# Issuing the value products of two attention steps together, with four probability buffers

## The reference

```
q, k, v = split(x @ Wq.T + bq), split(x @ Wk.T + bk), split(x @ Wv.T + bv)
q_stp = q @ Wqs.T + bqs
cross_kv = cross(k @ Wks.T + bks, v @ Wvs.T + bvs)
scores = (einsum('bhqd,bhkd->bhqk', q, k) + einsum('bhqc,bhkc->bhqk', q_stp, cross_kv)) * temp
attn = softmax(scores, axis=-1)
out = einsum('bhqk,bhkd->bhqd', attn, v)
```

## Time and profile before

| | us |
|---|---|
| median of 3 runs | 3909.57 |
| the profiled execution | 3902.91 |
| its span, first to last instruction | 3900.8 |
| TensorE matmul busy | 3424.4 (88%) |
| VectorE busy | 2953.6 (76%) |
| ScalarE busy | 2202.5 (56%) |
| GpSimd busy | 1521.5 (39%) |

### The profile page before, as it was taken

The page is one execution under the profiler, slowest core; times in us unless marked ns, Lnnn a source line. Parts: engine busy times, 40 slices in busy tenths (PEclk is TensorE's granted clock), DMA queues, the critical chain, the costliest instruction groups (busy, mean ns, idle before and its releaser), DMA issues. The chain is left out here.

```text
span 3900.8 us, 50068 instructions
## 1 busy us (share of the span) xinstructions
PE 3424.4 (88%) x14561; PEld 1588.6 (41%) x14561; DVE 2953.6 (76%) x3565; ACT 2202.5 (56%) x3624; POOL 1521.5 (39%) x1294
## 2 busy tenths in 40 slices
PE   3238989898898979889988999999999999999898
PEld 1114545455454545546542333323323333333566
DVE  3898787887878788796337888888878888887343
ACT  3436455554646555463215777777777777776221
POOL 0988778787878887797100000000000000000110
PEclk8669999899999989999998999999999999999999
DMA  2111213122121311223301000000000000001010
GB/s 97 33 33 54 60 57 106 57 76 73 55 82 57 106 57 58 69 75 105 107 19 66 18 18 18 18 19 20 22 16 21 18 18 18 18 18 34 22 32 27
DMA packets 110809, 183.02 MB, mean 47 GB/s; under 512 B 14608, under 2 KB 84648, under 8 KB 101866
## 3 DMA queue, kind: packets, MB, share of 16 engines
q1 hardware_dynamic: 110569, 180.13, 14.7%
HBM read 153.99 MB, written 26.09 MB: 46 GB/s over the span
## 5 line engine op out<-in xcount | busy, mean ns | idle before, releaser
L1830 DVE TENSOR_REDUCE tile_max<-ps 128x1 f32<-128x1024 f32 x1028 | 1211.4, 1220 | 246.4 <-PE ps L1621 243.6
L1771 ACT ACTIVATE probs<-ps 128x512 f32<-128x512 f32 x2056 | 1116.1, 598 | 372.4 <-PE ps L1635 346.7
L1373 POOL TENSOR_TENSOR vals<-vals,c_sb 128x512 f32<-128x512 f32 x512 | 685.0, 1369 | 321.7 <-DVE state L1182 321.6
L1176 DVE TENSOR_TENSOR_SCAN vals<-stacks,state,ps 128x512 f32<-128x512 f32 x512 | 655.1, 1280 | 105.9 <-POOL heads_v L1384 36.1
L1635 PE MATMUL ps<-stacks 101*128 101x512 bf16 x2056 | 708.8, 383 | 3.0 <-ACTq L1778 1.7
L1384 POOL TENSOR_TENSOR heads_v<-heads_v,vals 128x512 f32<-128x512 f32 x512 | 638.4, 1278 | 8.7 <-issue 0.2
L1621 PE MATMUL ps<-stacks 99*128 99x512 bf16 x2056 | 615.3, 380 | 0.0
L1645 PE MATMUL ps<-probs,heads_v 128*32 128x512 f32 x4096 | 546.3, 605 | 3.5 <-issue 3.5
L231 POOL COPY heads_v<-vals 128x256 f32 (+1 forms) x32 | 12.6, 400 | 1364.0 <-PE ps L1645 1329.0
L694 PE MATMUL ps<-x1T,e_w 128*128 128x512 f32 x1024 | 489.8, 626 | 58.6 <-ACT hid L968 58.6
L717 PE MATMUL ps<-e_w,hid 128*128 128x256 f32 x2048 | 458.5, 383 | 37.3 <-issue 18.2
(11 more groups left out here) (181 smaller groups left out, 2961.3 us busy)
## 6 DMA issues: line engine op xcount, KB each, us to landing
e_w<-in_e_w SPq DMA_DIRECT2D x64, 1024.0 KB, 7.1
c_sb<-scratch_c SPq DMA_DIRECT2D x128, 256.0 KB, 3.5
stacks<-scratch_q SPq DMA_DIRECT2D x210, 64.0 KB
stacks<-scratch_k SPq DMA_DIRECT2D x210, 64.0 KB
scratch_q<-parts SPq DMA_DIRECT2D x16, 384.0 KB, 4.2
scratch_k<-parts SPq DMA_DIRECT2D x16, 384.0 KB, 4.2
xr<-scratch_x SPq DMA_DIRECT2D x10, 512.0 KB, 4.2
xn_tok<-in_x SPq DMA_DIRECT2D x8, 512.0 KB, 4.8
```

What stands on the lines that cost most here:

```text
L1176: v.tensor_tensor_scan(h[:, n % 2, m, :], decay[:, n % 2, m, :], ps[:, 0, :], state[:, n, m:m + 1], ALU.mult, ALU.add).then_inc(s["h_ready ...
L1373: last = nc.gpsimd.tensor_tensor(h[:, n % 2, m, :], h[:, n % 2, m, :], c_sb[:, n % C_RING, :], ALU.mult)
L1771: fn(probs[:, step % 2, qc, :], ps[:, S_BANK[i], :], ACT.Exp)\
L1830: v.tensor_reduce(tile_max[:, t, half:half + 1], ps[:, slot(side):slot(side) + PAIR, :].rearrange("p a n -> p (a n)"), AX.X, ALU.max).then ...
```

## The change

The value products of steps s-2 and s-1 are issued together behind the scores of step s, for every even s, and those of steps 14 and 15 behind step 0 of the next head. `probs` gets four buffers, and the exponentials of a step wait for the value product of four steps before. The counter `av_mm` begins at 2, and the three other waits on it are raised by 2.

```diff
+PROBS = 4
+AV_CREDIT = 2
...
-        probs = sb("probs", [P, 2, QC, CH])
+        probs = sb("probs", [P, PROBS, QC, CH])
...
-                              probs[:, step % 2, qc, :], start=step == 0, stop=step == KT - 1)
+                              probs[:, step % PROBS, qc, :], start=step == 0, stop=step == KT - 1)
...
+            pe.sem_inc(s["av_mm"], AV_CREDIT)
...
-                    values(u, j, 0)
                     for step in range(2, KT):
                         at = turn_use(step, 0)
                         step_of(u, r, j, step, base + at, (M_BASE + at) % 2)
                         if step == TURN_STEP:
                             turn_max(base + TURN_USE, (M_BASE + TURN_USE) % 2, u + 1)
-                        values(u, j, step - 1)
+                        if step % 2 == 0:
+                            values(u, j, step - 2)
+                            values(u, j, step - 1)
...
                     step_of(u + 1, turn, after, 0, base, M_BASE % 2)
+                    values(u, j, KT - 2)
                     values(u, j, KT - 1)
...
-                at_least(act, s["av_mm"], u * KT + step - 1)
+                at_least(act, s["av_mm"], u * KT + step - PROBS + 1 + AV_CREDIT)
...
-                    fn(probs[:, step % 2, qc, :], ps[:, S_BANK[i], :], ACT.Exp)\
+                    fn(probs[:, step % PROBS, qc, :], ps[:, S_BANK[i], :], ACT.Exp)\
...
-                act.wait_ge(s["av_mm"], (u + 1) * KT)
+                act.wait_ge(s["av_mm"], (u + 1) * KT + AV_CREDIT)
...
-                wait_alone(pool, s["passed_pool"], s["av_mm"], (u - ROT + 1) * KT)
+                wait_alone(pool, s["passed_pool"], s["av_mm"], (u - ROT + 1) * KT + AV_CREDIT)
```

## The result

The changed kernel takes 3974.69 us, the median of 4 runs (3964.45 to 3979.27), against 3911.07 (4 runs, 3905.14 to 3913.17): a ratio of 1.0162, 95% interval 1.0136 to 1.0187. The change makes the kernel 1.6% slower; 3980 was predicted.

A forecast was written before the change was run, and what follows sets the result against it. TensorE was taken to set the pace, VectorE second at 83%. Pair losses sum to 2.19 us a head, 70 us over 32 heads: 3902.9 + 70 = 3973, 3980 as a median; range 3957 to 3993.

The forecast's parts named there:

- plain pair: Two back-to-back steps without transposes, five pairs a head: 5.93 us against 5.68, 0.25 slower, with waits of 0.18 and 0.27.
- pair (15, 0'): Step 15 with step 0 of the next head, waiting for a score bank: 5.96 us against 5.88, 0.08 more.
- pair (1,2): Steps 1 and 2, with the transpose of the values: ends at 6.80 us against 6.56 now, 0.24 more.
- join of two value products: On TensorE, each turn from pass to pass taken as 0.455 us; gain 0.20 a pair, 51 us in all.
- rival with a dear join: Each second value product costs the full exit, 0.54 for 0.455: 22 us more, 4002; chance 0.10.
- allowance for a cheap join: In the forecast's range: a turn between the two value products at 0.43 us takes 6 us off.
- pair (7,8): Steps 7 and 8, with the transpose of the row maxima: ends at 6.81 us, 0.62 more.
- the two errors named for it: In the range: 0.05 us a pair in the delays between engines, 13 us; the join at 0.43, 6 us off.
- Faster: Rival: the maxima banks come free in time, the waits vanish and the 51 us stay: 3859; chance 0.06.
- M0b and M2b: Second step's first products into each pair of maxima banks, predicted to wait 0.18 and 0.27 us for VectorE.
- The clock: Rival: TensorE's pauses lower its granted clock for 6% of the time, 45 us more: 4025; chance 0.04.
- S0: First of a step's four score products on TensorE, from which the prediction counts the times of a step or pair.

The follow-up runs named there:

- Short maxima: Each tile maximum reads 512 of its 1024 columns: on the changed kernel 3855.61 us, ratio 0.9848; on the kernel before 3886.36 us, ratio 0.9926.
- short exponentials: Changed kernel with 14 of 16 steps' exponentials done for 256 of 512 columns: 3974.63 us, ratio 1.0147 to the kernel before.
- deeper buffers: Kernel before with only the four probability buffers and the later wait of the exponentials, TensorE's order kept: 3917.31 us, ratio 1.0001.
- the transposes behind it: Kernel before with a head's two transposes issued behind the value product instead of in front of it: 3889.60 us, ratio 0.9936.

## Why the prediction was right

**What bounds the kernel, and the sign: right.** TensorE sets the pace before; back to back, the steps outrun VectorE. Short maxima turned the sign, short exponentials and deeper buffers did nothing.

**The waits of a plain pair: right to some 0.02.** Predicted 0.18 and 0.27, measured 0.18 and 0.25. VectorE's four maxima in a row and its 1.26 without work (1.3 predicted) are there too. The pair (15, 0') was put at 5.96, and is 5.91 (value product 2519.62 to 2525.53); the pair (1,2) at 6.80, and is 6.75 (2525.53 to 2532.28).

**The join of two value products: sized too dear.** I took 0.455 for each turn of a pass. What still ran in three narrow windows shows the starts of the second, third and fourth pass of the group that begins at 2507.86:

```profile
2508.31 1.04 PE L1647 MATMUL ps<-probs,heads_v 128*32 128x512 f32 x8
...
2508.74 1.04 PE L1647 MATMUL ps<-probs,heads_v 128*32 128x512 f32 x8
...
2509.17 0.61 PE L1647 MATMUL ps<-probs,heads_v 128*32 128x512 f32 x4
```

The third pass is the first of the second value product. Only the first turn costs 0.45 (2507.86 to 2508.31); the next two cost 0.43 (2508.31 to 2508.74, and to 2509.17), the lower bound that I had named. The joined products hold TensorE for 1.85, not 1.91. This is 0.055 in each of 256 pairs, some 14 us too many in the sum, and the rival with a dear join falls with it. My allowance for a cheap join, 6 us, counted one turn at 0.43 where two are.

**The pair (7,8): a wait overlooked.** Predicted 6.81, measured 6.90 (2544.05 to 2550.95), in spite of the cheaper join. VectorE's rows:

```profile
2549.16 0.19 DVE L215 TENSOR_REDUCE row_max<-tile_max 128x16 f32<-128x32 f32 x1
2549.46 2.35 DVE L1835 TENSOR_REDUCE tile_max<-ps 128x1 f32<-128x1024 f32 x2
```

I let the third maximum start 0.04 before the row maximum ended, as one tile maximum overlaps the last by 0.08. It starts 0.11 behind its end. The program has a wait there: the third maximum is the first of another head and overwrites `tile_max`, so it waits until the row maximum has been taken (`max_ready`, in `max_pair` on VectorE), and the prediction left this out. Whether the wait makes the whole 0.11, or the short row maximum a part of it, no run separates. From the pair's first score (2545.91) that is 3.55, not 3.41, and the transpose goes at 4.83 (2550.74) instead of 4.69. 0.14 in 32 heads is some 4 us too few.

**The sum.** A head takes 48.98 (2501.97 to 2550.95), predicted 49.2. The stage grew by 62.1 from first score to last, predicted 70. The two terms, 14 too many and 4 too few, make 10 of it; the 2 the other way are 0.01 in each of the 160 plain pairs, which is as fine as the rows can be read. For an execution like the profiled one 3973 was forecast and 3964.45 measured, 8.5 too many. That the median of 3980 lies only 5 above the measured one is in part luck: the changed kernel's profiled execution lay 10.2 below its median, that of before 6.7. The range of 3957 to 3993 held it, though its lower end is further off than the two errors named for it add up to (13 and 6, which is 3961).

**The rivals.** *Faster* needed the waits at M0b and M2b to vanish; they stand, and the run with short maxima shows what would have been had without them: 28.9 us against the same maxima in the single order. It is not the 51 of the prediction, because a wait of 0.11 for a score bank is next, and because the pair (15, 0') waits for its score banks in any case: it takes 5.91 there too (2532.69 to 2538.60), a little more than the 5.88 of the single order. *The clock* stayed at 1.00.

**The pages.** The Trainium skill (TensorEngine Tiling (Array Packing), Key Properties) says that a change of tiling mode drains TensorE. The rows agree: each exit measures 0.54 (S0 at 2509.71 behind the last pass at 2509.17) where a pass takes 0.43, and each entry 0.09, together 0.2, which the joined products pay once instead of twice. The change between bf16 and f32 products, which comes with it, is not what costs: with the transposes behind it, the value product still takes 1.00 until an untiled f32 product can start (2517.01 to 2518.01), and in the kernel before with short maxima an f32 transpose follows a bf16 score by 0.22, with nothing lost (2505.13 to 2505.35). What decided was the other side, the banks that VectorE had to free. The Trainium skill (the same page, PSUM Bottleneck) warns that tiling speeds up TensorE but not the evacuation of PSUM, and gives no size for it. The prediction says that the trace agrees, and that is more than its rows can show: the products whose maxima VectorE takes are not tiled, and no run compares tiled with untiled ones.

## What to carry to other kernels

A long operation between two bursts is not only a cost: if it gives a slower neighbour time to catch up, joining two of them can make bursts that the buffers between the engines don't carry. Compare the burst's issue time with the neighbour's work in it, buffer by buffer, before counting the switches saved; here 3.5 us of products met 4.6 us of reductions with two pairs of banks between them. The same view shows a gain: put the long operation in front of the instruction that waits (the transposes), and 21 us come off without a new buffer.

## What the runs showed of the hardware that was not expected

Of the four f32 passes of two joined value products, the first turn takes 0.45 and the two following 0.43 each, also the one from one value product's weights and probabilities to the next one's. So the extra 0.02 belongs to the beginning of the group and not to a change of operands.

A tile maximum directly behind another starts 0.08 before the first one's end. Behind the row maximum, which takes 0.19 and on which the program makes it wait, it starts 0.11 after the end: from one start to the next (2549.16 to 2549.46) that is 0.30. A short reduction with a wait behind it cost VectorE more of its time than its duration shows.
